# Attention: query and key heads in 16 rows each, three blocks of projections in place of six, scores as two chains of 64 rows

## The reference

```python
h = layernorm(x) * ln1_g + ln1_b
q, k, v = split(h @ in_proj_w.T + in_proj_b)           # 192 channels each: 12 heads of 16
p = softmax(q_head @ k_head.T / sqrt(16))              # 82 x 82 for each sequence and head
x = x + concat(p @ v_head) @ out_proj_w.T + out_proj_b
```

## Time and profile before

| | |
|---|---|
| median of 3 runs | 1385.61 us (1384.7 to 1394.42) |
| span of the profiled execution | 1385.7 us |
| PE busy | 1219.3 us (88%) |
| DVE busy | 1016.9 us (73%) |
| ACT busy | 690.1 us (50%) |
| POOL busy | 745.5 us (54%) |
| attention, first scores to last scores | from 821.2 to 1064.3 us |

### The profile page before, as it was taken

One profiled execution on the slowest core, in us unless ns is written; L12 is line 12 of the kernel. 1 busy time (PEld: TensorE's weight loads), 2 busy tenths in 40 slices (PEclk: granted clock), 3 DMA queues, 4 the chain that ended last, 5 costly groups with the idle time before them and its releaser, 6 DMA issues.

```text
span 1385.7 us, 19455 instructions
## 1 busy us (share of the span) xinstructions
PE 1219.3 (88%) x5828; PEld 782.3 (56%) x5829; DVE 1016.9 (73%) x1934; ACT 690.1 (50%) x1467; POOL 745.5 (54%) x469
## 2 busy tenths in 40 slices
PE   7996767477998989898987789999999999999996
PEld 4342334133454545454552458888888677777774
DVE  5899696998998989999999745788879653333332
ACT  1147431776767676777756235555543332222221
POOL 3037670877888786969697320135545564222222
PEclk9798868798999999999999999999999699999998
DMA  6200001440404040322320001112222132222221
GB/s 183 58 1 0 31 9 47 169 147 1 146 0 147 1 145 27 120 63 83 108 71 1 0 9 58 42 49 73 59 62 82 39 63 46 36 37 37 35 35 21
DMA packets 72799, 81.17 MB, mean 59 GB/s; under 512 B 13282, under 2 KB 64705, under 8 KB 72721
## 3 DMA queue, kind: packets, MB, share of 16 engines
q1 hardware_dynamic: 53386, 69.29, 16.0%
q0 software_dynamic: 17152, 9.24, 5.0%
q10 hardware_dynamic: 2184, 1.72, 0.5%
HBM read 48.87 MB, written 30.01 MB: 57 GB/s over the span
## 4 chain that ended last, share of the span: by engine, by line
PE 59%; DVE 20%; ACT 10%; issue 6%; POOL 2%; DMA 1%; DVEq 0%; SPq 0%; ACTq 0%; POOLq 0%
PE ps L2239 10%; PE ps L2258 6%; PE ps L1021 6%; DVE hs L1305 6%; PE ps L1623 3%; PE ps L1681 3%; PE ps L932 3%; PE ps L257 3%; PE ps L250 3%; PE ps L1696 2%; ACT ps L1174 2%; PE ps L2248 2%; PE ps L998 2%; PE ps L957 2%; ACT prod L378 2%
## 5 line engine op out<-in xcount | busy, mean ns | idle before, releaser
L1423 POOL TENSOR_TENSOR Bx<-dtz,Bb 128x984 f32<-128x984 f32 x128 | 289.5, 2281 | 45.0 <-DVE hs L1305 31.2
L1305 DVE TENSOR_TENSOR_SCAN hs<-ps,Bx 128x492 f32<-128x492 f32 x256 | 287.7, 1165 | 22.1 <-POOL Bx L1423 12.8
L1174 ACT ACTIVATE ps<-dt,A 128x324 f32<-128x324 f32 (+1 forms) x512 | 211.5, 456 | 79.5 <-DVE hs L1305 77.3
L1021 PE MATMUL ps<-hs,b_id 128*128 128x492 f32 x512 | 238.5, 588 | 12.0 <-DVE y L1272 9.3
L2358 POOL DMA_INDIRECT out<-yt,dest x48 | 74.7, 1556 | 170.8 <-DVE yt L2344 158.2
L1315 DVE TENSOR_TENSOR hs<-hs,ps 128x984 f32<-128x984 f32 x128 | 150.3, 1174 | 2.5 <-issue 0.5
L2239 PE MATMUL ps<-W,xT 97*128 (+1 forms) x384 | 143.7, 518 | 3.1 <-issue 2.0
L1021 PEld LDWEIGHTS ps<-hs,b_id 128*128 128x128 f32 x512 | 92.9, 195 | 79.7 <-issue 74.3
L2328 DVE COPY hT__5717<-ps 128x768 f32<-128x768 f32 x48 | 46.0, 958 | 112.1 <-PE ps L2248 110.7
L2296 ACT ACTIVATE hb<-ps 128x768 f32<-128x768 f32 x48 | 38.9, 811 | 143.3 <-PE ps L2239 143.3
L2258 PE MATMUL ps<-W,hT__5717 128*128 x576 | 109.3, 327 | 0.8 <-DVE yb L2338 0.8
(11 more groups left out here) (277 smaller groups left out, 2402.2 us busy)
## 6 DMA issues: line engine op xcount, KB each, us to landing
Bb<-b_rows SPq DMA_DIRECT2D x32, 656.0 KB, 7.1
buckets<-b_zero SPq DMA_DIRECT2D x8, 2288.0 KB, 15.4
xg<-buckets SPq DMA_DIRECT2D x48, 104.0 KB, 2.0
xc<-in_xcol SPq DMA_DIRECT2D x4, 1176.0 KB, 9.6
W<-in_w1d SPq DMA_DIRECT2D x8, 582.0 KB
W<-in_w2d SPq DMA_DIRECT2D x8, 576.0 KB
out<-H SPq DMA_DIRECT2D x8, 246.0 KB
H<-P SPq DMA_DIRECT2D x8, 147.0 KB
```

The lines of the kernel that those rows point to most:

```text
L1021: mm = pe.matmul(ps[:, BANK_Y + h, 0:HALF], ident[:], f2(hs[:, s % LONG])[:, h * HALF:(h + 1) * HALF], start=s == 0, stop=s == STATE - 1)
L1174: a = act.activation(ps[:, BANK_A + h, c:c + w].rearrange("p (g t) -> p g t", t=S)[:, :, 1:S], dt[:, (par + t // STATE) % 2, m, g0 * S:g1 ...
L1305: v.tensor_tensor_scan(f2(hs[:, t % LONG])[:, c], ps[:, BANK_A + h, 0:HALF], f2(Bx[:, t % RING])[:, c], 0.0, ALU.mult, ALU.add).then_inc(s ...
L1423: g.tensor_tensor(Bx[:, t % RING], dtz[:, p], Bb[:, p, t % STATE, :].rearrange("p (a n) -> p a n", a=1).broadcast_to([128, NI, N]), ALU.mu ...
```

## The change

`_shared` and the plain slices of the weights put heads at 16 rows each. Block Q0 holds the queries of heads 0 to 7, block K0 their keys, and block QK the rest: queries of heads 8 and 9, their keys, queries of heads 10 and 11, their keys, 32 rows each. That is 3 blocks of projections in place of 6.

`keep_keys` now takes all 128 rows four times with a scale of one or zero by row (`V_KM`, made by `_only`) and a bias that is zero in the same rows (`V_KB`), so that of each group of four heads one remains; nothing of `kB0` needs a memset. `keep_others` does block QK in six instructions of 32 rows, and moves the keys to the partitions of the queries they belong to; the rows that they leave in `qT` and `kB1` are zero from memsets. The scores are four matmuls of 64 rows: on rows 0 to 63 heads 0 to 3 and 8, 9 go to the first bank, on rows 64 to 127 heads 4 to 7 and 10, 11 to the second. The order of heads in `E` and `PT` is then that of `HEAD_AT`, and the product with V reads them so.

`SIDE_TILES` has 12 places in place of 14, one of them empty.

```diff
+HEAD_AT = (0, 1, 2, 3, 8, 9, 4, 5, 6, 7, 10, 11)
...
-    BANKS = {"RT0": 0, "RT1": 1, "Q0": 2, "Q1": 3, "Q2": 0, "K0": 1, "K1": 2, "K2": 3, "V0": 0, "V1": 1}
+    BANKS = {"RT0": 0, "RT1": 1, "Q0": 2, "K0": 3, "QK": 0, "V0": 1, "V1": 2}
...
-        g.memset(kB[:], 0.0).then_inc(s_cst, 1)
+        g.memset(kB[:, :, 4 * N:6 * N], 0.0).then_inc(s_cst, 1)
+        g.memset(qT[:, :, 1, :], 0.0).then_inc(s_cst, 1)
...
     def keep_queries(act, j, par, place):
-        for m_ in range(3):
-            act.wait_ge(s_q, j * 3 + (m_ + 1))
-            act.activation(qT[:, par, m_, :], ps[:, place(f"Q{m_}"), 0:N], ACT.Identity, bias=qb[:, m_:m_ + 1],
-                           scale=0.25).then_inc(s_qT, 1)
-
-    def keep_keys(act, j, par, m_, place):
-        act.wait_ge(s_k, j * 3 + (m_ + 1))
+        act.wait_ge(s_q, j + 1)
+        act.activation(qT[:, par, 0, :], ps[:, place("Q0"), 0:N], ACT.Identity, bias=qb[:, 0:1], scale=0.25).then_inc(s_qT, 1)
+
+    def keep_keys(act, j, par, place):
+        act.wait_ge(s_k, j * 2 + 1)
         for h in range(4):
-            c = slice(32 * h, 32 * h + 32)
-            a = act.activation(kB[c, par, m_, :, h, :], ps[c, place(f"K{m_}"), 0:N].rearrange("p (g s) -> p g s", g=G),
-                               ACT.Identity, bias=vec[c, V_KB + m_:V_KB + m_ + 1])
+            a = act.activation(kB0[par][:, :, h, :], ps[:, place("K0"), 0:N].rearrange("p (g s) -> p g s", g=G),
+                               ACT.Identity, bias=vec[:, V_KB + h:V_KB + h + 1], scale=vec[:, V_KM + h:V_KM + h + 1])
+        a.then_inc(s_kT, 1)
+
+    def keep_others(act, j, par, place):
+        act.wait_ge(s_k, j * 2 + 2)
+        for first in (0, 64):
+            q, k = slice(first, first + 32), slice(first + 32, first + 64)
+            act.activation(qT[q, par, 1, :], ps[q, place("QK"), 0:N], ACT.Identity, bias=qb[q, 1:2], scale=0.25)
+            for h in range(2):
+                a = act.activation(kB1[par][q, :, h, :], ps[k, place("QK"), 0:N].rearrange("p (g s) -> p g s", g=G),
+                                   ACT.Identity, bias=vec[k, V_K2B + h:V_K2B + h + 1], scale=vec[k, V_K2M + h:V_K2M + h + 1])
         a.then_inc(s_kT, 1)
...
                 fr.project(pe, "Q0", 0, fr.s_q)
-                fr.project(pe, "Q1", 1, fr.s_q)
-                fr.project(pe, "Q2", 2, fr.s_q)
-                fr.project(pe, "K0", 3, fr.s_k)
+                fr.project(pe, "K0", 1, fr.s_k)
+                fr.project(pe, "QK", 2, fr.s_k)
                 post(last, 1, 12, None)
                 post(last, 1, 13, None)
-                pe.wait_ge(fr.s_qT, 2)
-                fr.project(pe, "K1", 4, fr.s_k)
-                fr.project(pe, "K2", 5, fr.s_k)
...
-                      ("Q0", FRONT, s_qT, 3, 1), ("Q1", FRONT, s_qT, 3, 2), ("Q2", FRONT, s_qT, 3, 3), ("K0", FRONT, s_kT, 3, 1),
-                      ("LG", NEWS, s_L, 1, 1), ("K1", FRONT, s_kT, 3, 2), ("K2", FRONT, s_kT, 3, 3),
-                      ("V0", FRONT, s_V, 2, 1), ("V1", FRONT, s_V, 2, 2)]
+                      ("Q0", FRONT, s_qT, 1, 1), ("K0", FRONT, s_kT, 2, 1), ("LG", NEWS, s_L, 1, 1), ("QK", FRONT, s_kT, 2, 2),
+                      ("V0", FRONT, s_V, 2, 1), ("V1", FRONT, s_V, 2, 2), (None, None, None, 0, 0)]
...
                 if q == 1:
                     pe.wait_ge(s_x2T, j * 2 + 2)
-                    for m_ in range(3):
-                        project(f"Q{m_}", m_, s_q, j)
-                    project("K0", 3, s_k, j)
+                    project("Q0", 0, s_q, j)
+                    project("K0", 1, s_k, j)
                 if q == 2:
-                    project("K1", 4, s_k, j)
-                    project("K2", 5, s_k, j)
+                    project("QK", 2, s_k, j)
...
-                    for h0, h1 in ((0, 4), (4, 6), (6, 8), (8, 12)):
-                        m_, j = h0 // 4, h0 % 4
-                        mm = pe.matmul(ps[0:S, SCORES + h0 // 6, (h0 % 6) * S:(h0 % 6 + h1 - h0) * S],
-                                       qT[:, par, m_, q * S:(q + 1) * S], kB[:, par, m_, q, j:j + h1 - h0, :].rearrange("p h s -> p (h s)"),
-                                       start=True, stop=True)
+                    for a, keys, m_, h0, h1 in ((0, kB1, 1, 4, 6), (1, kB0, 0, 0, 4), (0, kB0, 0, 0, 4), (1, kB1, 1, 4, 6)):
+                        half = slice(64 * a, 64 * a + 64)
+                        mm = pe.matmul(ps[0:S, SCORES + a, h0 * S:h1 * S], qT[half, par, m_, q * S:(q + 1) * S],
+                                       keys[par][half, q].rearrange("p h s -> p (h s)"), start=True, stop=True)
                     mm.then_inc(s_s, 1)
```

More of the change, by code:

```diff
@@ L77 @@
 V_QB = 114
-V_KB = 117
-V_ROW = 120
-V_H_NORM = 121
-V_HF_NORM = 123
-V_N = 125
+V_KM = 116
+V_KB = 120
+V_K2M = 124
+V_K2B = 126
+V_ROW = 128
+V_H_NORM = 129
+V_HF_NORM = 131
+V_N = 133
 CH = 4
@@ L709, in scale_bias @@
     def scale_bias(act):
-        act.activation(qb[:], vec[:, V_QB:V_QB + 3], ACT.Copy, scale=0.25).then_inc(s_qb, 1)
+        act.activation(qb[:], vec[:, V_QB:V_QB + 2], ACT.Copy, scale=0.25).then_inc(s_qb, 1)
         act.wait_ge(s_qb, 1)
@@ L1596, in _ @@
         def _(pe):
[L1597 removed]
+            pe.wait_ge(s_cst, 5)
             pe.wait_ge(s_V, 2)
@@ L1694, in step @@
                     at_least(pe, s_x3, i * G + (q - 3))
-                    for h in range(HEADS):
-                        mm = pe.matmul(ps[0:S, HEAD_OUT + c % 2, h * (DH + 1):(h + 1) * (DH + 1)], PT[:, c % 2, h, :], V[:, vpar, c, h, :],
+                    for n, h in enumerate(HEAD_AT):
+                        mm = pe.matmul(ps[0:S, HEAD_OUT + c % 2, h * (DH + 1):(h + 1) * (DH + 1)], PT[:, c % 2, n, :], V[:, vpar, c, h, :],
                                        start=True, stop=True)
@@ L1764, in front @@
                     fr.keep_queries(act, j, par, bank)
-                for m_ in {1: (0,), 2: (1, 2)}.get(q, ()):
-                    fr.keep_keys(act, j, par, m_, bank)
+                    fr.keep_keys(act, j, par, bank)
+                if q == 2:
+                    fr.keep_others(act, j, par, bank)
             def route(i, par, q):
@@ L2411, in _haar, with _shared, _only @@
     return np.where(odd % 2 == 1, -0.0625, 0.0625).astype(np.float32)
-def _heads(a):
+def _shared(q, k):
     import numpy as np
-    a = np.asarray(a).reshape(12, 16, -1)
-    out = np.zeros((12, 32, a.shape[2]), a.dtype)
-    out[:, 0:16] = a
-    return out.reshape(384, -1)
+    return np.concatenate([q[128:160], k[128:160], q[160:192], k[160:192]])
+def _only(a, size, number):
+    import numpy as np
+    p = np.arange(128)
+    return np.stack([np.where(p % (size * number) // size == n, a, 0) for n in range(number)], axis=1).astype(np.float32)
 def _layout(x):
@@ L2459, in _layout @@
     wq, wk, wv = t["ffn_in_proj_w"].reshape(3, 192, 192)
-    a["w_qk"] = rows(np.concatenate([_heads(wq), _heads(wk)]), 96).reshape(96, 2, 6, 128)
+    a["w_qk"] = rows(np.concatenate([wq[0:128], wk[0:128], _shared(wq, wk)]), 96).reshape(96, 2, 3, 128)
     a["w_v"], a["w_ao"], a["w_r"] = rows(wv, 96), rows(t["ffn_out_proj_w"], 96), rows(t["ffn_router_w"], 96)
```

42 lines of the change are left out of this document (22 added, 20 removed).

## The result

The changed kernel takes 1417.75 us (median of 4 runs, 1403.93 to 1428.23), the kernel before 1385.15 beside it. The ratio is 1.0213, with a 95% interval from 1.0158 to 1.0267: it is slower, and whether by more than 2% isn't settled. The prediction was 1380 with a range from 1348 to 1403. It named the right mechanism, falls of the clock that eat what the change saves, and made them far too small.

The account below looks back on a forecast made before the run. PE was taken to bound attention, with DVE near it and binding the changed round. Savings of 35.8 us from 1385.7 gave 1350 with the clock held; six clock falls of 5 us gave back 30: 1380 us, range 1348 to 1403.

Parts of the forecast that it names:

- Scores of a sequence, 1.13 us: Attention's score block: 64-row chains overlap, 0.83 plus 0.30 us for the halves, against 1.66 now, saving 0.53 a sequence.
- the 0.30 of the pair: Cost of going into the halves and out, read from two 64-row matmuls of `pair` (L935): 1.95 us against 1.65.
- No overlap (the last rival): Half-row score chains don't overlap: scores 1.96 us a sequence, no new falls, 1369 us in all; chance 0.07.
- The round at full clock, 29.3 us: Attention round of four sequences, quarter 2 to quarter 2, bound through DVE's chain: 29.3 us, 3.6 less than 32.9.
- The idle before XS, 2.2 us: PE would wait some 2.2 us for DVE's copy before turning the normed rows in quarter 1 of a round.
- The start, 1.9 us: Before attention, in the scan's tail, two projections go; 1.9 of their 2.4 us saved, since the last product needs `av`.
- The reading of the fall at 1019: The one clock fall in the old rounds, 3.0 us, followed scores, turn and narrow V multiplies with only 0.24 us idle.
- a fall costs 5 us, six times, 30 in all: One clock fall in each of six rounds that turn XS, 10 us at half clock each, giving back 30 of 36.
- The sum without the clock: Savings with the clock held: 14.4 steady, 14.4 early, 2.1 last round, 1.9 start, 3.0 old fall; 35.8 us, giving 1350.
- The rival of long falls: PE stays at 1.2 GHz some 17 us of each round until quarter 3's values, 8.5 x 6 = 51 us: 1401; chance 0.20.
- The rival of a held clock, 1350: The clock stays at full rate through attention or falls once or twice: 1350 us, or up to 6 more; chance 0.22.
- the 36 us under the forecast: Whole saving at held clock, 35.8 us, from attention's rounds and its start, of which falls would give back 30.

Follow-up runs that it names:

- e7: Kernel before with three blocks of projections, full-height scores, and each pass with V over up to four heads' columns (68 for 17); ratio 0.9993, 1380.56 us.
- e9: Kernel before with the experts' second weights W2 loaded as one piece of 4608 bytes a partition in place of six of 768; ratio 0.9990.
- e1 to e5: Before with three blocks; before with half-row scores; changed with 68-column V passes; before with those; changed with projections repeated: ratios 1.0009, 1.0136, 1.0026, 0.9977, 1.0165.
- the wide product: Each pass with V takes up to four heads' columns, 68 in place of 17, same result; alone on the kernel before, ratio 0.9977.

## Why the prediction was wrong, point by point

- **Scores of a sequence, 1.13 us: 0.99.** Both halves' passes start together and run as two chains, and going in and out costs 0.99 - 0.83 = 0.16, not the 0.30 of the pair. The row was taken from a place with other shapes; the sign and the choice against 1.66 + 0.30 were right. No overlap (the last rival) is out.
- **The round at full clock, 29.3 us: right where it can be seen.** No round ran at full clock from end to end, but its parts did. From the scores of quarter 2 to those of quarter 1 17.94 was forecast, 908.53 - 890.33 = 18.20 measured; from the turn of XS to the next quarter 2 8.06 forecast, 957.87 - 949.63 = 8.24 measured. **The idle before XS, 2.2 us: 1.33** and 0.59, put down to DVE's copy, as said.
- **The start, 1.9 us: some 1.7.** Attention starts 4.2 us earlier (817.0 for 821.2), but 0.9 us of this stand already at Mamba's last passes of L1021, which start at 776.3 before and at 775.4 after (L1035 there). From these to the first scores it is 44.9 us before and 41.7 after, and a fall of the clock in between lasts 10.2 us before and 6.8 after. With the fall of 10.2 us three blocks take 43.3 (e7), 1.6 less than six; with that of 6.8 us six blocks take 43.4 (e9), 1.7 more than three. The rest is chance: over the runs' profiles attention starts anywhere from 811.9 to 821.9.
- **The reading of the fall at 1019.** The 0.24 us of idle PE that I put ahead of it is that of another round, at 956.22, and stands behind the product with V; the 7 us before 1019 show 6.93 us busy and no wait as long.
- **The term that failed: a fall costs 5 us, six times, 30 in all.** The sum without the clock makes attention 243.1 - (35.8 - 1.9) = 209.2 us; it took 278.3. By this sum the falls cost 69, 8.6 us each, and past 6.0 the kernel turns slower, as the prediction says. (The 209.2 are an estimate: no run has the halves and a clock that holds.) There were eight, from 3.4 to 68.3 us long and 20.7 in the mean, where six of 10 were forecast. Two steps led there. I took the fall's length from the two falls of the kernel before, and behind the one in the rounds came full-height scores and, in quarter 1, eight more wide passes of projections; the change removes these, and I allowed only 3 us for that. And I let idle be the cause: "PE at half speed is no longer ahead of DVE, so the idle that causes the fall shrinks in the next round" was my argument against the rival with long falls. The idle did shrink (none before the turn of XS inside that fall), but the clock stayed down: in the row of 68.30 us PE is busy throughout at 0.50. A round at this clock takes 1006.71 - 957.87 = 48.8 us from quarter 2 to quarter 2, where the forecast has 29.3 and 5 for the fall. What moved the clock in the experiments is what the passes carry: 64-row passes, 17-column passes, fewer projections (e1 to e5). Short waits of PE may still start a fall where the passes are thin: six of the eight falls have one of 0.24 to 1.84 us in the 7 us before them. No run settles this.
- **The rival of long falls** was the closest, 1401, and too small as well: it let the clock come back with the values of quarter 3, and they and the projections behind them run inside the 68.30 us at 0.50.
- **The rival of a held clock, 1350, was out of reach, and so was the 36 us under the forecast.** The sum took it that a shorter attention shortens the kernel. I read PE, DVE and ACT and not SP's queue, whose first gather goes out 2.5 us before the last scores. With the clock held, e7 kept at most 1.4 us of its 21.7 (medians 1380.56 and 1381.93), which isn't clear of noise; the 1380 forecast added up a gain that couldn't be had and a loss that was too small.
- **The rule on idle gaps.** The Trainium skill ("TensorE: Matmul & The Clock Gate", Why this matters for your kernels) lets the clock drop after idle gaps between matmul bursts that are longer than any here, and by it the clock would have held. The trace of the changed kernel disagrees: the longest idle time of PE in front of one of its falls is 1.84 us (it ends at 820.64), and in the rounds that turn XS 1.33.

## What to carry to other kernels

Before counting on a shorter stage, look at who else ends with it: follow the issuing queue to the stage's last transfer, and divide a transfer's bytes by its time (26 GB/s was one engine here; 97 rows became 96 and 1). When fp32 passes are split over halves of rows or made fewer and narrower, read the granted clock before and after, and over several runs: PE's busy share is 88% in both kernels and doesn't tell it. Where more moving columns cost a pass no time, as the product with V shows, they can make the clock fall less often.

## What the runs showed of the hardware

- TensorE stayed at 1.2 GHz for 68.30 us with PE busy 68.30 us. With the wide product, attention had 0 to 17 us at that clock with full-height scores and 58 to 110 with 64-row scores. This was shown by exchange of the passes; by which quantity the chip decides wasn't measured.
- 24 fp32 passes of 82 x 82 weights take 1.87 us with 17 and with 68 moving columns, at full clock.
- Two chains of 64-row passes on the two halves of the rows run side by side: a sequence's scores take 0.99 us where full height takes 1.66, and 1.87 at half clock.
- A load of 97 rows ran at 26 GB/s with a DMA share of 0.07, about one engine of 16, and held the queue behind it: some 25 us for a pair of 1158 KB. As 96 and 1 the eight pairs are issued in 31 us and move at 239 GB/s. The size of the pieces (768 or 4608 bytes) made no difference as long as the 97 rows were there.
